# Attention heads sorted to partitions by transfers instead of turns on TensorE, with a new written order of steps

## Chip, core, metric

One NeuronCore of a Trainium2 chip runs the whole program in one launch. The metric is the device time in microseconds of that launch. The engines are TensorE (PE, matmuls; PEld is its weight load), VectorE (DVE), ScalarE (ACT), GpSimd (POOL) and SyncE (SP), which here only issues DMAs.

## What is computed

Two layers over x of shape 4 x 512 x 128 (batch, tokens, channels). Each layer normalizes x and adds an attention and a feed-forward branch to it. Cut to what matters:

```python
xn = _layernorm(x)
x = x + L0_attn(xn) + L0_ffn(xn)     # L0_ffn: ln, causal attention, residual, ln, mixture of 8 experts (128 -> 512 -> 128)
xn = _layernorm(x)
x = x + L1_attn(xn) + L1_ffn(xn)     # L1_attn: not causal; L1_ffn: 8 experts (128 -> 128 -> 128), top 2
# each attention, 16 heads of 8 channels:
scores = einsum('bhqd,bhkd->bhqk', q, k) / sqrt(8)      # causal in the first two
attn = softmax(scores)
out = einsum('bhqk,bhkd->bhqd', attn, v)                # heads side by side: 128 channels
out = out @ w_out
```

So there are 3 attentions for each of 4 batch elements, 12 in all, named (b, u) here: u = 0 is L0_attn, u = 1 the attention inside L0_ffn (both causal), u = 2 is L1_attn.

## The kernel before

Everything stays in SBUF between load and store. The channels or the keys lie on the 128 partitions, 512 tokens on the free axis (TILES = 4 tiles of 128). Heads are handled in four quads of four; quads 2n and 2n + 1 share one accumulation, a pair.

A step is a tuple such as ("max", b, u, g, i, k). The string SCORE is an order written out by hand: each letter takes the next step of one of 13 chains, a digit gives its PSUM bank. `plan` unrolls it, and every engine walks through the same list in order and executes its part of each step; semaphores join the parts. The letters: A the front of a batch element (norms, turns, projections, L84), K stacking q and k for the score matmuls (SP's DMAs, L1075) and loading the experts, M the scores whose maximum VectorE takes (L484, L810), T the turn of these maxima and their DMA into q_stack (max_turn, L833, L497, L1103), S scores and their exp (L840, L717), V values (L857), H the steps on heads, F the middle of a batch element (norms, routing, projections of u = 2), G gates and the store, E and O the layer-0 experts in and out, I and J those of layer 1.

One attention after its scores: the values step (L857) multiplies the exps by v_ones, whose 25 columns for each head are 8 values, a column of ones and zeros (the odd head of a pair comes 16 rows lower). So sum_bank, bank 7, fills with 8 unnormalized values and the sum of exps for each of 8 heads. ScalarE copies it to head_sums (L738) after the second quad of the pair. Then the H steps:

- heads_turn, once for each pair: four TensorE transposes of head_sums (L884); VectorE takes reciprocals of the sums (L511) and multiplies them in (L515) into heads.
- heads_back, once for each attention: four transposes of heads (L892); VectorE copies them to headsT (L520).
- out_project: four matmuls with the output weights (L899), added by VectorE (L530).

Each matmul or transpose of 32-bit numbers shows as two instructions in the trace's timeline when a group is merged (x8 for four), except for transposes.

ScalarE does exp for scores (L730) and gelu for experts (L754); it loads a table (ACT_TABLE_LOAD) whenever it changes from one function to the other.

SP's queue holds, in the order of the plan: loads of x, the stacking DMAs (up to 12 of 128 KB for one attention, L1095 and L353), the max_turn copies (L1108, 32 KB each), the stores (L1114).

## Time and profile before

| | |
|---|---|
| runs of the program | 780.64, 783.39, 783.80 us; median 783.39 |
| the profiled execution | 779.85 us |
| its span, first to last instruction | 778.0 us |
| TensorE granted clock, mean | 0.99 |
| instructions | 16113 |
| DMA packets, bytes | 34427, 31.70 MB |

Busy shares overlap in time, since the engines run side by side. The chain of work is followed back from the last instruction, at each step to what released it. Where an engine sat idle, the profile names what ended the wait. "issue" is time for which the profile shows no wait.

### The profile page before, as it was taken

How to read it: one execution, taken by the hardware profiler on the slowest of the kernel's cores; microseconds unless marked ns; L12 is line 12 of the kernel's file. 1: busy time of each engine (PE TensorE's matmuls, PEld its weight loads, DVE VectorE, ACT ScalarE, POOL GpSimd, SP SyncE). 2: the span in 40 equal slices, each digit the busy share in tenths (PEclk: the TensorE clock that was granted, in tenths of full speed). 3: DMA queues.
4: the chain of work that ended last, by engine and by line, in shares of the span. 5: the costliest groups of instructions: out<-in, count | busy, mean ns of one | idle time of the engine just before them, and what ended most of it. 6: DMA issues, size and time to landing. Idle time of an engine off the chain costs nothing.

```text
span 778.0 us, 16113 instructions
## 1 busy us (share of the span) xinstructions
PE 730.4 (94%) x6352; PEld 400.1 (51%) x6352; DVE 586.6 (75%) x1161; ACT 499.7 (64%) x623; POOL 181.4 (23%) x421
## 2 busy tenths in 40 slices
PE   3687999999999999999999999999999999999998
PEld 2332455677535366556444446566544566743344
DVE  5896996466999887477898887764898743579984
ACT  5374765566687566756777764746687683377784
POOL 5163553012432002112451200020552000010000
PEclk9799999999999999999999999999999999999999
DMA  5364230000200200030120110030030000011000
GB/s 136 78 192 168 71 79 16 3 19 3 77 19 11 67 17 3 18 88 5 52 61 3 49 44 3 3 91 3 19 93 4 3 1 3 1 51 44 16 5 14
DMA packets 34427, 31.70 MB, mean 41 GB/s; under 512 B 10184, under 2 KB 33616, under 8 KB 33872
## 3 DMA queue, kind: packets, MB, share of 16 engines
q1 hardware_dynamic: 32624, 29.09, 13.4%
q10 hardware_dynamic: 1728, 1.57, 0.9%
q8 instruction: 51, 0.84, 0.5%
q14 instruction: 24, 0.20, 0.1%
HBM read 7.32 MB, written 1.05 MB: 11 GB/s over the span
## 4 chain that ended last, share of the span: by engine, by line
PE 74%; DVE 11%; ACT 9%; DMA 3%; issue 2%; ACTq 0%; SPq 0%; POOL 0%; DVEq 0%; POOLq 0%
PE psum L950 17%; PE psum L937 14%; PE psum L872 14%; PE psum L824 8%; PE psum L851 8%; DVE neg_max L492 6%; ACT probs L754 3%; PE psum L803 3%; ACT L754 2%; ACT probs L730 2%; ACT L730 2%; DMA q_stack<-maxT 1%; PE psum L806 1%; PE psum L829 1%; PE psum L884 1%
## 5 line engine op out<-in xcount | busy, mean ns | idle before, releaser
L492 DVE TENSOR_REDUCE neg_max<-psum 128x2 f32<-128x1024 f32 (+2 forms) x320 | 344.9, 1111 | 87.2 <-PE psum L829 59.7
L730 ACT ACTIVATE probs<-psum 128x1024 f32<-128x1024 f32 (+1 forms) x320 | 288.5, 938 | 118.2 <-PE psum L851 116.7
L872 PE MATMUL psum<-probs,v_ones 128*25 128x512 f32 (+3 forms) x1536 | 152.3, 494 | 0.1
L754 ACT ACTIVATE probs<-psum,col 128x512 f32<-128x512 f32 x160 | 98.8, 688 | 53.3 <-PE psum L937 52.9
L824 PE MATMUL psum<-k_stack,q_stack 64*128 64x512 bf16 (+3 forms) x768 | 114.9, 331 | 15.4 <-ACT probs L730 4.2
L950 PE MATMUL psum<-ew,probs 128*128 128x128 f32 x1024 | 128.6, 279 | 0.0
L950 PEld LDWEIGHTS psum<-ew,probs 128*128 128x128 f32 x1024 | 120.3, 192 | 15.8 <-issue 13.5
L851 PE MATMUL psum<-q_stack,k_stack 64*128 64x512 bf16 (+3 forms) x768 | 108.2, 328 | 10.5 <-DMA q_stack<-maxT 4.9
L937 PE MATMUL psum<-normed_T_a,ew 128*128 128x512 f32 x256 | 117.2, 597 | 0.0
L1031 POOL TENSOR_SCALAR_AFFINE_SELECT probs<-probs 128x512 f32<-128x512 f32 x128 | 80.9, 640 | 145.7 <-ACT probs L730 144.1
L653 DVE SCALAR_TENSOR_TENSOR acc<-psum,gate,acc 128x128 f32<-128x128 f32 x256 | 72.1, 344 | 36.1 <-PE psum L950 32.3
L1017 POOL CAST max_part<-neg_max 128x16 bf16<-128x16 f32 x48 | 9.4, 196 | 352.2 <-DVE neg_max L492 352.1
L824 PEld LDWEIGHTS psum<-k_stack,q_stack 64*128 64x128 bf16 x768 | 37.1, 94 | 88.1 <-DVE neg_max L492 22.0
L851 PEld LDWEIGHTS psum<-q_stack,k_stack 64*128 64x128 bf16 x768 | 32.1, 94 | 76.0 <-ACT probs L730 25.3
L937 PEld LDWEIGHTS psum<-normed_T_a,ew 128*128 128x128 f32 x256 | 45.6, 190 | 46.2 <-issue 39.9
L754 ACT ACT_TABLE_LOAD x29 | 37.2, 1283 | 32.9 <-PE psum L937 32.7
L872 PEld LDWEIGHTS psum<-probs,v_ones 128*25 128x25 f32 x1536 | 33.5, 103 | 48.1 <-issue 31.5
L829 PEld LDWEIGHTS psum<-above,pick 64*128 64x128 bf16 x1024 | 44.4, 96 | 16.8 <-issue 1.0
L829 PE MATMUL psum<-above,pick 64*128 64x64 bf16 x1024 | 51.8, 192 | 0.0
L730 ACT ACT_TABLE_LOAD x26 | 33.4, 1283 | 26.0 <-PE psum L851 25.8
L950 PE MATMUL psum<-wout,probs 128*128 128x128 f32 x256 | 35.4, 283 | 0.5 <-ACT probs L754 0.5
L950 PEld LDWEIGHTS psum<-wout,probs 128*128 128x128 f32 x256 | 30.9, 191 | 8.2 <-issue 5.2
(126 smaller groups left out, 569.5 us busy)
## 6 DMA issues: line engine op xcount, KB each, us to landing
q_stack<-part SPq DMA_DIRECT2D x72, 128.0 KB, 2.4
k_stack<-part SPq DMA_DIRECT2D x60, 128.0 KB, 2.5
ew<-w_expert_in SPq DMA_DIRECT2D x1, 2048.0 KB, 8.1
ew<-w_expert_out SPq DMA_DIRECT2D x1, 2048.0 KB, 12.5
q_stack<-k_stack SPq DMA_DIRECT2D x14, 128.0 KB, 2.3
k_stack<-part ACTq DMA_DIRECT2D x12, 128.0 KB, 3.9
q_stack<-maxT SPq DMA_DIRECT2D x48, 32.0 KB, 1.9
x_in<-x SPq DMA_DIRECT2D x4, 256.0 KB, 3.4
```

Of the source, the lines that this page charges most:

```text
L492: eng.tensor_reduce(neg_max[:, q % 2, :, xs[0]:xs[-1] + 1, i], src, AX_X, ALU.max, negate=True).then_inc(vector_done.sem, 1)
L653: eng.scalar_tensor_tensor(out=acc_of[b % 2][:, t, :], in0=src[:, t * P:(t + 1) * P], scalar=gate_of[layer][:, t, expert:expert + 1], in1= ...
L730: eng.activation(dst, src, ACT.Exp, scale=SCALE).then_inc(probs_ready.sem, 1)
L754: ins = eng.activation(probs[:, order.slot[step[:-1]], 2 * k + f, :], two_banks(step)[:, f, :], ACT.Gelu_apprx_tanh if layer else ACT.Gelu ...
L803: ins = eng.matmul(dst, proj_qk[:, u, k, :], src[:, :], start=True, stop=True)
L824: ins = eng.matmul(dst[:, a, col0:col0 + keys], q_stack[slot][rows_of, head, i * P:(i + 1) * P], k_stack[slot][rows_of, head, 0:keys], sta ...
L829: ins = eng.matmul(dst[:, a, col0:col0 + HALF], pick[rows_of, upper, :], above[rows_of, upper, :], start=False, stop=upper == 1)
L851: ins = eng.matmul(dst[:, a, n * width:(n + 1) * width], k_stack[slot][rows_of, head, j * P:(j + 1) * P], q_stack[slot][rows_of, head, TIL ...
L872: ins = eng.matmul(sum_bank[32 * c:32 * c + V_COLS, q0:TILES * P], v_ones[u][:, j, g // 2 * QH + c, col0:col0 + V_COLS], probs[:, order.sl ...
L937: ins = eng.matmul(dst[:, f, :], w, normed_T["y" if layer else "a"][:, :], start=True, stop=True)
L950: ins = eng.matmul(dst[:, t * P:(t + 1) * P], middle[:, f, t * P:(t + 1) * P], w, start=f == chunks[0], stop=f == chunks[-1])
L1031: eng.affine_select(out=diagonal, in_=diagonal, compare_op=ALU.is_ge, fill=no_chance, base=0, pattern=[[0, QH], [1, P]], channel_multiplie ...
```

## The change

The turns of heads go. The columns of v_ones are laid out anew: each head has 16 rows of the sum bank (VALUE_ROWS), its 8 values at even rows and its sum of exps at row 1; 32 columns are loaded for each head (V_COLS) instead of 25, and the rows that it doesn't own are zeros. With that, values and sums of all heads lie at even strides over the partitions, and transfers can sort them:

- heads_sort, once for each pair: SP issues two DMAs from head_sums, the sums into heads_den (64 partitions x 64) and the values into heads_raw (64 partitions x 512, already in the order of channels).
- heads_inverse, once for each attention: VectorE waits for both pairs' sorts and takes one reciprocal over heads_den, 128 x 64.
- heads_write and heads_read: SP writes heads_den to a scratch in DRAM (16 x 512) and reads it back with each row spread over 8 partitions, into heads_inv (128 x 512).
- heads_norm: VectorE waits for the read and multiplies heads_raw by heads_inv into headsT.
- out_project is as before.

ScalarE's copy to head_sums now waits for the sorts of two pairs before. SCORE is written anew throughout; H has 84 steps instead of 48, the other chains have the same steps as before. The diff, without the string:

```diff
-SUM_COL, ODD_ROW = HD, 16
-ODD_COL = SUM_COL + 1 + ODD_ROW
-V_COLS, PAIR_COLS = ODD_COL, ODD_COL + SUM_COL + 1
+VALUE_ROWS, SUM_COL = 2 * HD, 1
+V_COLS, PAIR_COLS = 2 * VALUE_ROWS, 3 * VALUE_ROWS
...
-        heads += [("heads_turn", b, u, pair) for pair in range(QUADS // 2)] + [("heads_back", b, u), ("out_project", b, u)]
+        heads += [("heads_sort", b, u, 0), ("heads_sort", b, u, 1), ("heads_inverse", b, u), ("heads_write", b, u),
+                  ("heads_read", b, u), ("heads_norm", b, u), ("out_project", b, u)]
...
-        heads = sb("heads", [P, TILES, P])
-        inv_sum = sb("inv_sum", [P, TILES, 2 * QH])
+        heads_raw = sb("heads_raw", [P, TILES * P])
+        heads_den = sb("heads_den", [P, HALF])
+        heads_inv = sb("heads_inv", [P, TILES * P])
+        inverses = nc.dram_tensor("inverses", [HEADS, TILES * P], F32).ap()
...
-                        dst = v_ones[u][:, :, :, ODD_COL * odd:ODD_COL * odd + HD]
+                        dst = v_ones[u][:, :, :, V_COLS * odd:V_COLS * odd + VALUE_ROWS:2]
...
-                elif kind == "heads_turn":
-                    eng.wait_ge(vector_done.sem, vector_done.n)
-                    eng.reciprocal(inv_sum[:, :, :], src[:, :, :, SUM_COL]).then_inc(vector_done.sem, 1)
-                    eng.wait_ge(vector_done.sem, vector_done.count())
-                    eng.tensor_tensor(dst, src[:, :, :, 0:HD], inv, ALU.mult).then_inc(vector_done.sem, 1)
-                elif kind == "heads_back":
-                    eng.tensor_copy(headsT[:, :], bank(step)).then_inc(vector_done.sem, 1)
+                elif kind == "heads_inverse":
+                    n_heads = ATTENTIONS.index(step[1:])
+                    for pair in range(QUADS // 2):
+                        eng.wait_ge(heads_landed[pair].sem, 32 * (n_heads + 1))
+                    eng.reciprocal(heads_den[:, :], heads_den[:, :]).then_inc(vector_done.sem, 1)
+                elif kind == "heads_norm":
+                    eng.wait_ge(inverses_read.sem, 16 * (ATTENTIONS.index(step[1:]) + 1))
+                    eng.tensor_tensor(headsT[:, :], heads_raw[:, :], heads_inv[:, :], ALU.mult)\
+                       .then_inc(vector_done.sem, 1)
...
-                        eng.wait_ge(work_full.sem, order.work["heads_turn", *order.head_pairs[q - 2]] + 1)
+                        eng.wait_ge(heads_landed[q % 2].sem, 32 * (q // 2))
...
-                        col0 = (SUM_COL + 1) * (g % 2)
+                        col0 = VALUE_ROWS * (g % 2)
...
-                elif kind == "heads_turn":
-                    for t in range(TILES):
-                        ins = eng.transpose(dst[:, t * P:(t + 1) * P], head_sums[:, q % 2, t * P:(t + 1) * P],
-                                            ident[:, :])
-                elif kind == "heads_back":
-                    for t in range(TILES):
-                        ins = eng.transpose(dst[:, t * P:(t + 1) * P], heads[:, t, :], ident[:, :])
...
+                elif kind == "heads_sort":
+                    u, pair = step[2:]
+                    q = order.head_pairs.index((b, u, pair))
+                    if q >= 2:
+                        eng.wait_ge(vector_done.sem, order.dve["heads_norm", *ATTENTIONS[q // 2 - 1]])
+                    eng.wait_ge(scalar_done.sem, order.act["values", b, u, 2 * pair + 1, TILES - 1])
+                    rows_of = slice(HALF * pair, HALF * pair + HALF)
+                    for dst, src in ((heads_den, head_sums[SUM_COL:P:VALUE_ROWS, q % 2, :]),
+                                     (heads_raw, head_sums[0:P:2, q % 2, :])):
+                        eng.dma_start(dst[rows_of, :], src).then_inc(heads_landed[pair].sem, 16)
+                        heads_landed[pair].count()
+                elif kind == "heads_write":
+                    eng.wait_ge(vector_done.sem, order.dve["heads_inverse", *step[1:]])
+                    eng.dma_start(inverses, heads_den[:, :]).then_inc(inverses_written.sem, 16)
+                    inverses_written.count()
+                elif kind == "heads_read":
+                    eng.wait_ge(inverses_written.sem, 16 * (ATTENTIONS.index(step[1:]) + 1))
+                    eng.dma_start(heads_inv[:, :], inverses.unsqueeze(1).to_broadcast([HEADS, HD, TILES * P]))\
+                       .then_inc(inverses_read.sem, 16)
+                    inverses_read.count()
```

## Rows read from the trace of the kernel before

**Rows 1.** The page, part 1: busy us, share of span, instructions.

```profile
PE 730.4 (94%) x6352; PEld 400.1 (51%) x6352; DVE 586.6 (75%) x1161; ACT 499.7 (64%) x623; POOL 181.4 (23%) x421
```

**Rows 2.** The chain that ended last, shares of the span: engines, then lines.

```profile
PE 74%; DVE 11%; ACT 9%; DMA 3%; issue 2%; ACTq 0%; SPq 0%; POOL 0%; DVEq 0%; POOLq 0%
...
PE psum L950 17%; PE psum L937 14%; PE psum L872 14%; PE psum L824 8%; PE psum L851 8%; DVE neg_max L492 6%; ACT probs L754 3%; PE psum L803 3%; ACT L754 2%; ACT probs L730 2%; ACT L730 2%; DMA q_stack<-maxT 1%; PE psum L806 1%; PE psum L829 1%; PE psum L884 1%
```

**Rows 3.** Windows: PE, PEld, DVE, ACT, POOL busy us (instructions); clock, DMA share, GB/s.

```profile
0.00:40.00 40.00, 20.10 (x164) 11.28 (x164) 28.77 (x68) 18.05 (x35) 14.07 (x44) 0.87 0.46 109
...
80.00:120.00 40.00, 39.16 (x512) 19.61 (x515) 38.35 (x72) 28.83 (x37) 20.73 (x42) 1.00 0.26 68
```

**Rows 4.** Groups by form: busy us, mean ns of one | idle before.

```profile
L950 PE MATMUL psum<-ew,probs 128*128 128x128 f32 x1024 | 128.6, 279 | 0.0
...
L653 DVE SCALAR_TENSOR_TENSOR acc<-psum,gate,acc 128x128 f32<-128x128 f32 x256 | 72.1, 344 | 36.1 <-PE psum L950 32.3
...
L515 DVE TENSOR_TENSOR heads<-psum,inv_sum 128x256 f32<-128x256 f32 x24 | 10.2, 424 | 0.8
L511 DVE RECIPROCAL inv_sum<-psum 128x32 f32<-128x32 f32 x24 | 8.6, 357 | 9.9 <-PE psum L884 7.7
L520 DVE COPY headsT<-psum 128x512 f32<-128x512 f32 x12 | 8.2, 684 | 2.4 <-PE psum L892 2.4
```

**Rows 5.** VectorE's prices: groups by form, and line 594 (min/median/max ns).

```profile
L492 DVE TENSOR_REDUCE neg_max<-psum 128x2 f32<-128x1024 f32 x192 | 228.5, 1218 | 43.8 <-PE psum L824 25.1 <-PE psum L829 17.0
...
L417 DVE TENSOR_TENSOR acc<-x_bias,a_sum 128x512 f32<-128x512 f32 x4 | 2.7, 680 | 0.0
...
L594 DVE RECIPROCAL gate_t<-gate_s x4: 177/178/179, 214.2 to 742.5; 128x4 f32<-128x4 f32 x4
```

**Rows 6.** Pieces of the chain in order: start us, us, what.

```profile
92.64 0.59 PE psum L892 x4
...
112.76 0.61 DVE headsT L520
```

**Rows 7.** Weight loads: two groups by form, and one piece of the timeline.

```profile
L872 PEld LDWEIGHTS psum<-probs,v_ones 128*25 128x25 f32 x1536 | 33.5, 103 | 48.1 <-issue 31.5 <-POOL probs L1031 4.1 <-ACT probs L730 2.2
...
L790 PEld LDWEIGHTS psum<-ident,normed_a 128*128 128x128 f32 x16 | 1.7, 140 | 2.9 <-DVE normed_a L408 2.9
...
767.03 0.12 PEld L872 LDWEIGHTS psum<-probs,v_ones 128*25 128x25 f32 x4 [0.30 <-issue]
```

**Rows 8.** Groups: ScalarE's table loads ahead of gelu.

```profile
L754 ACT ACT_TABLE_LOAD x29 | 37.2, 1283 | 32.9 <-PE psum L937 32.7
```

**Rows 9.** Line 1108's issue (ns) and landing; then KB each, median us to landing.

```profile
L1108 SPq DMA_DIRECT2D q_stack<-maxT x48: 531/532/1263, 33.1 to 756.3; - x48
...
DMA to landing us min/median/max: 1.8/1.9/10.7
...
k_stack<-part SPq DMA_DIRECT2D x60, 128.0 KB, 2.5
...
q_stack<-maxT SPq DMA_DIRECT2D x48, 32.0 KB, 1.9
x_in<-x SPq DMA_DIRECT2D x4, 256.0 KB, 3.4
out<-acc SPq DMA_DIRECT2D x4, 256.0 KB, 2.6
```

**Rows 10.** The chain's end, in order of time: start us, us, what.

```profile
765.80 3.61 PE psum L872 x32
...
769.43 0.61 ACT head_sums L738
...
772.43 0.89 PE psum L950 x8
...
773.36 1.14 PE psum L899 x8
...
774.60 0.69 DVE acc L530
```

86 lines of the change are left out of this document (38 added, 48 removed).

## Prediction

> **What bounds the kernel now.** I read the busy shares first. TensorE is busy 730.4 us of 778.0 (94%), VectorE 75%, ScalarE 64% [rows 1]. Then the chain that ended last: 74% of it lies on TensorE, 11% on VectorE, 9% on ScalarE, 3% on DMA [rows 2]. So an instruction taken from TensorE's queue has about three chances in four of shortening the run. The stretches show where not: in the first 40 us TensorE is busy 28.77 us, held by loads and by the first chain of norm, projection and stacking, which the change leaves as it is; from 80 to 120 us VectorE is busy 38.35 of 40 us and TensorE merely follows it [rows 3]. The rest of the run is TensorE's, with small waits for PSUM banks.
>
> The profiled execution took 779.85 us, for a span of 778.0; the median of the runs shown is 783.39, a factor of 1.0045. The sum is made against 779.85 and multiplied by that factor at the end.
>
> **TensorE work removed.** Each of the 12 attentions turns its sums twice (L884, four transposes each) and its heads back once (L892): 24 + 12 = 36 groups. Four transposes take 0.59 us of the chain where nothing delays them [rows 6], so 36 x 0.59 = 21.2 us of TensorE's time go, and nothing on TensorE replaces them. Are they on the path? Going through the chain piece by piece, 28 of the 36 groups are on it, for 15.7 us, the tail's among them; [rows 6] has the first of L892's. The tail I count apart, so 14.4 us are proven on the path of the old order and at most 33 x 0.59 = 19.5 us can be had before the tail. The order is written anew around the missing groups, so I take 17, nearer the middle. **Term: -17 (-14.4 to -19.5).**
>
> **VectorE work.** Removed: 24 reciprocals of 0.357, 24 products of 0.424, 12 copies of 0.684 = 8.6 + 10.2 + 8.2 = 27.0 us [rows 4]. Added for each attention: one reciprocal over 128x64 and one product over 128x512. Reciprocals take 178 ns for 4 elements and 357 for 32 [rows 4, 5], 6.4 ns an element, so 0.56 us for 64; a tensor-tensor of 128x512 in SBUF takes 0.68 [rows 5]. 12 x 1.24 = 14.9 us. VectorE is relieved by 12.1 us. Its removed pieces lie on the chain for only 2.5 us (such as the 0.61 of headsT, [rows 6]), so at the same share the added work costs 1.4. **Term: -1.1 (-12.1 if VectorE ruled everywhere; 0 if hidden).** The copies into v_ones now write every second element; from their row's 24 instructions I see no reason for more than a few tenths of a us in all.
>
> **Wider value columns.** Weight loads for values go from 25 to 32 columns. 25 columns take 103 ns, 128 columns of the transposes 140 [rows 7], so 7 columns are 2.5 ns and 1536 loads 3.9 us. In a step of 512 queries they are hidden: after each four loads the loader idles 0.30 us [rows 7]. Only the narrow causal steps can show it. The matmuls stream the same queries. **Term: +1 (0 to +3.9).** The larger clears of v_ones (1536 elements instead of 1088 for each partition) fall in the first 40 us, some tenths.
>
> **Table loads.** ScalarE reloads its table at every change between exp and gelu, 55 times at 1.28 us (29 ahead of gelu in [rows 8], 26 ahead of exp). Following the steps scores, gate_exp and expert_in through both orders, the changes number 55 before and 49 after. On the chain the table loads (the pieces of L754 and L730 without a tile's name) stand with 2% each of 778 us, 2.1 and 1.6% before rounding: 29 us [rows 2], 0.52 us each, so six fewer give **-3.1 (0 to -7.7).**
>
> **The transfers, between the attentions.** The turns of an attention are replaced by six DMAs: two sorts for each pair of quads, one write, one read, all issued from SP. Issuing one holds SP 0.53 to 0.6 us [rows 9]; 72 more are some 43 us of a queue that is mostly waiting. None is nothing in time to landing: the sort of values moves 128 KB between SBUF rows as k_stack<-part does (2.5 us), the sort of sums and the write are small (32 KB of maxT in rows of 256 bytes takes 1.9; a write to DRAM, out<-acc, 2.6), the read of 256 KB is like x_in<-x (3.4) [rows 9]; I take 2.2 for the write and 2.9 for the read, a little below these rows since only the data of 32 KB come from DRAM. From the last values step to heads_inverse: copy 0.60, one issue 0.6 ahead of the second sort, landing 2.5: 3.7 us. From heads_inverse to heads_norm: 0.56 + 2.2 + 2.9 and three hand-overs of 0.1, about 5.9 us. VectorE executes in order, so what it has between these steps in the new order is the cover. By mean durations of its rows (a max over 1024 is 1.22, an expert's accumulation 72.1 / 64 = 1.13, [rows 4, 5]) the cover is, for the first gap and the second: attention (0,1) 4.1 and 5.5; (1,1) 3.6 and 4.9; (3,1) 3.6 and 5.6; (0,0) 5.3 and 6.5; (2,2) 4.5 and 10.0; (2,1) 14 and 8.4; (2,0) has 2.6 in the first gap, but two expert_in steps of TensorE pass there too, and 30 in the second; the four others have at least 5.4 and 11.5. So three attentions lack up to 1 us in each gap, the others next to nothing. ScalarE may reach the copy behind an exp of 1 us. A stall of VectorE at heads_inverse or heads_norm holds all max reductions behind it, and TensorE waits for their banks. **Term: +2.5 (0 to +12)**: the high end is each of the three transfers landing 1 us later at five attentions, most of it on the path.
>
> SP also executes in order. heads_write waits for VectorE and heads_read for the write's landing, and behind them stand max_turn copies, which scores wait for: behind the read of (0,1) and the write of (0,2) at once. These copies must pass a wait of about 2 us; scores of that quad follow several steps later. The old trace has such a wait once at its start (the DMA of maxT behind others: 10.7 us at worst against 1.9, [rows 9]), so the price is inside the +12 and no term of its own.
>
> The Trainium skill, "DMA: Bandwidth & Descriptors", sections "Specifications" and "Anatomy of one DMA", speaks against this change: rows under 512 B go through a read-modify-write, and completion is slowest where the target is HBM. The new sums and the scratch move in rows of 256 bytes, and the scratch is HBM. The trace does not show much of it: maxT's 256-byte rows land in 1.9 us, and the store to DRAM in 2.6. With the page's figure of about 2.0 us fixed for any DMA, an estimate from that page puts the three landings at 6 us instead of my 7.6 and the gaps' term near 0.
>
> **The tail.** Before: the last values end at 769.4 and the last sum at 775.3, 5.9 us [rows 10]. After, by the same rows and those above: copy 0.61, issue 0.6, sort 2.5, inverse 0.56, write 2.2, read 2.9, product 0.68, output projection 1.14, sum 0.69, six hand-overs of 0.1: 12.5 us, so +6.6. But seven expert_out steps stand behind the last values step instead of one, and a route_turn too: 6 x 0.97 + 0.44 = 6.3 us of TensorE work that ran before it; 81% of such work is on the chain (L950: 17% of 778 is 132 us, of 128.6 + 35.4 busy in its two forms; [rows 2, 4]), so -5.1. VectorE has 8.7 us of work ahead of heads_norm in the tail, less than the 9.9 to that point, so the transfers set the end. **Term: +1.5 (0 to +5).**
>
> **Sum.** -17 - 1.1 + 1 - 3.1 + 2.5 + 1.5 = -16.2; 779.85 - 16.2 = 763.7; times 1.0045 = 767.1 us.
>
> **Rivals.** (a) *The new order gains more than it loses work.* VectorE's 12.1 us also count in the stretches it rules, the groups are all worth their 0.59 and the waits are covered: -19.5 for the groups, -5 for VectorE, -4 for tables and fewer bank waits, +2 = -26.5, 757 us. For it: 47.6 us of TensorE idle stand in [rows 1], for an order to use. Against it: 11 of these are in the first 40 us [rows 3], where a dependency holds. (b) *The gain turns into other waits.* VectorE and ScalarE end next; TensorE's place on the chain passes to max reductions (6% now) and exps. Then only VectorE's relief and the tables count: -1.1 - 3.1 and a third of the groups, -6, with +3 of waits: -7, 776 us with the factor. For it: stretches like 80 to 120 us. Against it: 28 of 36 groups on the chain. (c) *The round trip is too long: slower.* One mechanism: VectorE stands at heads_norm (and SP at heads_read) until write and read have landed. It costs nothing up to about 6 us and then its excess at each tightly placed attention: (1,1), (3,2), (0,1), (3,1), (0,0) and, from 8.4 us, (2,1). With write and read each at twice their nearest row it is 10.8 us; the covers of 4.9, 5.2, 5.5, 5.6, 6.5 and 8.4 us lack 28.7 us together, at 0.85 on the path 24 us. Without the term for waits the sum is -18.7, so the result is 785, with the factor 789 us. It decides from about 10 us. For it: no row has a read of DRAM right behind a write of it, and 128 rows of 256 bytes to DRAM are not in the trace; one maxT copy took 10.7 us when others were ahead. Against it: the medians, and that stacking bursts rarely coincide. (d) *The change doesn't do what it says*: the shorter work only moves slack, the new order holding TensorE at banks for as long as the turns took, within 4 us of before: 782 us.
>
> **How the numbers follow.** Forecast (762 to 772) 0.45; (a) 0.22; (b) 0.14; (c) 0.13; (d) 0.06. About 0.5% (4 us) is what a measurement of this kernel can tell from no change, so faster needs less than 779.5: forecast, (a), and most of (b), 0.79; same 0.09, slower 0.12. The range leaves out half of (c) and the far end of (a): 753 to 785.
>
> **What would show it.** L884, L892, the copy and the small reciprocals gone; TensorE busy near 709 us; VectorE near 575; 51 or fewer table loads in all; the new transfers at 2 to 3.4 us; VectorE's waits for DMA ahead of heads_inverse and heads_norm below 5 us in total; last values to the end about 12.5 us plus the store. A read of the scratch at over 5 us, or VectorE's DMA waits over 15 us, would make the prediction wrong on the slow side; a chain below 70% on TensorE would point to (b).

## Result and profile after: slower by half a per cent

The changed kernel takes 786.75 us (median of 16 runs, 784.37 to 790.83) against 783.17 for the kernel before on the same chip (16 runs, 780.64 to 785.1): a ratio of 1.0047 with a 95% interval of 1.0034 to 1.006. The forecast was 767.1 us in a range of 753 to 785, so both the sign and the range were missed. The profiled execution took 787.67 us for a span of 785.8, at a mean granted clock of 0.969; the one profiled of before had 0.99. Times in the following sections are medians, each with its ratio to runs of the kernel before on the same chip; a few executions, of the kernel before too, took 17% to 125% longer than the others and are left out.

**Time goes with the granted clock.** TensorE's granted clock differs from run to run. Of 77 runs of the kernel before that stood beside the experiments, the 16 at a mean of 0.975 or 0.976 took 784.0 to 785.9 us, the 5 at 0.990 or 0.991 took 779.6 to 780.0: about 3.3 us for 0.01. (The profiled run of before is one of the high ones, so its busy times are not quite comparable with those of the others, which lie near 0.98.) The median clock is 0.980 over the runs of before and 0.976 over those of the changed kernel. By an estimate from these runs that is some 1.3 of the 3.6 us between them; what follows shows where a part of the low clock comes from.

The first row of the page of the changed kernel, busy us of each engine:

```profile
PE 723.4 (92%) x6208; PEld 386.7 (49%) x6208; DVE 574.7 (73%) x1126; ACT 487.8 (62%) x617; POOL 182.3 (23%) x421
```

The chain that ended last, its shares by engine:

```profile
PE 68%; DVE 10%; ACT 9%; DMA 3%; issue 2%; POOL 0%; SPq 0%; ACTq 0%; DVEq 0%
```

The 144 transposes are gone (6352 instructions to 6208, [rows 1]), VectorE's busy time fell by 11.9 us as forecast (12.1), ScalarE's by 11.9. TensorE's fell by 7.0 only, to 723.4 us where the prediction looked for 709. The span grew by 7.8 all the same. TensorE's share of the chain fell from 74% [rows 2] to 68%.

**One place shows at once.** SP's timeline (start us, us, queue, line, what) has the load of the experts' weights, four DMAs, and eight us behind it, with seven stacking transfers in between, a copy of maxima:

```profile
68.24 0.58 SPq L1060 DMA_DIRECT2D ew<-w_expert_in  x1
68.88 0.44 SPq L1060 DMA_DIRECT2D ew<-w_expert_out  x1
69.36 0.43 SPq L1060 DMA_DIRECT2D win<-w_in  x1
69.84 0.58 SPq L1060 DMA_DIRECT2D wout<-w_out  x1
...
78.08 1.02 SPq L1114 DMA_DIRECT2D q_stack<-maxT  x1
```

The same place in its chain (start us, us, what):

```profile
78.08 11.99 DMA q_stack<-maxT
```

In its waits (engine and line <- for what: us in total, times, longest):

```profile
PE psum L854 <- DMA q_stack<-maxT: 11.8, 1, 11.8
```

Its windows there (busy us and instructions of PE, PEld, DVE, ACT, POOL; clock, DMA share, GB/s):

```profile
70.00:80.00 10.00, 8.22 (x117) 3.29 (x117) 8.99 (x12) 6.41 (x9) 6.46 (x15) 1.00 0.97 399
80.00:90.00 10.00, 0.00 (x0) 0.00 (x0) 0.00 (x0) 0.00 (x0) 0.00 (x0) 0.55 1.07 252
90.00:100.00 10.00, 9.58 (x121) 3.85 (x121) 7.64 (x9) 5.84 (x7) 3.26 (x8) 0.77 0.33 79
```

From 80 to 90 us no compute engine did anything at all. The DMA engines were full with 5 MB of weights and the stacking transfers issued behind them, and a copy of 32 KB that usually lands in 1.8 us took 12.0. The granted clock was 0.55 in this stretch and 0.77 in the ten us behind it. The kernel before has the same load and a copy of 10.7 us [rows 9], but the load is issued at 50.6 us there, between other work, and TensorE waited 4.9 us for the copy. The new order moved the load to stand ahead of the stacking for the next batch element and of the copy for quad (0,1,1).

**What grew elsewhere.** Five more of the changed kernel's waits:

```profile
ACT probs L733 <- PE psum L854: 124.9, 131, 14.0
ACT probs L757 <- PE psum L923: 75.7, 39, 8.7
DVE neg_max L499 <- PE psum L832: 69.7, 44, 12.4
DVE acc L653 <- PE psum L936: 66.7, 28, 9.3
...
ACT L757 <- PE psum L923: 45.1, 17, 7.8
```

The first three in the kernel before:

```profile
ACT probs L730 <- PE psum L851: 116.7, 146, 5.3
DVE neg_max L492 <- PE psum L829: 59.7, 38, 5.8
ACT probs L754 <- PE psum L937: 52.9, 31, 5.2
```

The fourth stood at 32.3 there [rows 4], the last at 32.7 [rows 8]. The waits of ScalarE and VectorE for the experts' matmuls (second, fourth and fifth) grew by 38% to 107%. The stall above is in none of these three (none of their single waits is as long as it); it is in the longest of the other two, 14.0 and 12.4 us.

**What the transfers took.** The changed kernel's DMA issues (KB each, median us to landing):

```profile
heads_inv<-inverses SPq DMA_DIRECT2D x12, 256.0 KB, 3.3
...
inverses<-heads_den SPq DMA_DIRECT2D x12, 32.0 KB, 1.5
```

Line 1102, the write:

```profile
DMA to landing us min/median/max: 1.4/1.5/2.5
```

The reciprocal of line 517 (ns, first and last start, form):

```profile
L517 DVE RECIPROCAL heads_den<-heads_den x12: 539/544/554, 92.6 to 774.2; 128x64 f32<-128x64 f32 x12
```

The wait for the sorted sums and values:

```profile
DVE heads_den L517 <- DMA heads_raw<-head_sums: 2.1, 3, 1.0
```

The round trip is 1.5 + 3.3 = 4.8 us (5.1 forecast), and VectorE waited 2.1 us in all at the inverses and 0.6 at heads_norm. In the output projections TensorE's matmuls waited 2.2 us for headsT and its weight loads 3.1.

### The profile page after: what moved, and what is told of

The parts are those of the page before. It is cut to its first block, busy times and chain, and to the rows that moved or that the text cites. A ratio compares the mean times of both kernels' runs of the same rounds, so it can differ in the third digit from the quotient of the medians.

```text
span 785.8 us, 15828 instructions
## 1 busy us (share of the span) xinstructions
PE 723.4 (92%) x6208; PEld 386.7 (49%) x6208; DVE 574.7 (73%) x1126; ACT 487.8 (62%) x617; POOL 182.3 (23%) x421
## 4 chain that ended last, share of the span: by engine, by line
PE 68%; DVE 10%; ACT 9%; DMA 3%; issue 2%; POOL 0%; SPq 0%; ACTq 0%; DVEq 0%
PE psum L936 18%; PE psum L923 15%; PE psum L875 13%; PE psum L827 7%; PE psum L854 7%; DVE neg_max L499 4%; ACT probs L733 3%; PE psum L806 3%; ACT probs L757 2%; ACT L757 2%; DMA q_stack<-maxT 2%; DVE acc L653 1%; PE psum L832 1%; ACT L733 1%; PE psum L809 1%
## 5 line engine op out<-in xcount | busy, mean ns | idle before, releaser
L875 PE MATMUL psum<-probs,v_ones 128*32 128x512 f32 (+3 forms) x1536 | 159.0, 505 | 0.0
L827 PE MATMUL psum<-k_stack,q_stack 64*128 64x512 bf16 (+3 forms) x768 | 117.8, 340 | 18.1 <-ACT probs L733 5.9
L854 PE MATMUL psum<-q_stack,k_stack 64*128 64x512 bf16 (+3 forms) x768 | 110.3, 334 | 20.0 <-DMA q_stack<-maxT 11.8
L936 PEld LDWEIGHTS psum<-ew,probs 128*128 128x128 f32 x1024 | 120.0, 192 | 15.0 <-issue 12.9
L936 PE MATMUL psum<-ew,probs 128*128 128x128 f32 x1024 | 126.9, 278 | 0.4 <-ACT probs L733 0.4
L854 PEld LDWEIGHTS psum<-q_stack,k_stack 64*128 64x128 bf16 x768 | 32.3, 94 | 96.4 <-ACT probs L733 29.7
L757 ACT ACT_TABLE_LOAD x24 | 30.8, 1283 | 45.3 <-PE psum L923 45.1
L875 PEld LDWEIGHTS psum<-probs,v_ones 128*32 128x32 f32 x1536 | 34.2, 109 | 46.9 <-issue 31.5
L832 PE MATMUL psum<-above,pick 64*128 64x64 bf16 x1024 | 53.6, 195 | 0.0
L982 POOL TENSOR_TENSOR rstd<-var_eps,minus_half 128x4 f32<-128x4 f32 x16 | 16.2, 1013 | 84.6 <-DVE var_eps L403 84.3
## 6 DMA issues: line engine op xcount, KB each, us to landing
ew<-w_expert_out SPq DMA_DIRECT2D x1, 2048.0 KB, 12.8
```

The source lines that it names most:

```text
L757: ins = eng.activation(probs[:, order.slot[step[:-1]], 2 * k + f, :], two_banks(step)[:, f, :], ACT.Gelu_apprx_tanh if layer else ACT.Gelu ...
L827: ins = eng.matmul(dst[:, a, col0:col0 + keys], q_stack[slot][rows_of, head, i * P:(i + 1) * P], k_stack[slot][rows_of, head, 0:keys], sta ...
L832: ins = eng.matmul(dst[:, a, col0:col0 + HALF], pick[rows_of, upper, :], above[rows_of, upper, :], start=False, stop=upper == 1)
L854: ins = eng.matmul(dst[:, a, n * width:(n + 1) * width], k_stack[slot][rows_of, head, j * P:(j + 1) * P], q_stack[slot][rows_of, head, TIL ...
L875: ins = eng.matmul(sum_bank[32 * c:32 * c + V_COLS, q0:TILES * P], v_ones[u][:, j, g // 2 * QH + c, col0:col0 + V_COLS], probs[:, order.sl ...
L936: ins = eng.matmul(dst[:, t * P:(t + 1) * P], middle[:, f, t * P:(t + 1) * P], w, start=f == chunks[0], stop=f == chunks[-1])
```

## Experiments

Three questions: was it the experts' load; was it the transfers; and what was the removed TensorE work worth at all?

**1. The experts' load earlier in the changed kernel.** Half of it goes out when the first keys have landed (22.5 us), half behind the first max_turn (31.9 us); its place in the order is the only other difference. This kernel is called version 1 below.

```diff
-        "K": stacks[:2 * PARTS] + [("load_experts", 0)] + stacks[2 * PARTS:],
+        "K": stacks[:PARTS] + [("load_experts", 0)] + stacks[PARTS:3] + [("load_experts", 1)] + stacks[3:],
...
-                    for dst, src in ((ew1[:, :, :, :], w_expert_in), (ew2[:, :, :, :], w_expert_out),
-                                     (win[:, :, :], w_in), (wout[:, :, :], w_out)):
+                    if b == 0:
+                        eng.wait_ge(keys_landed[0].sem, 96)
+                    for dst, src in (((ew1[:, :, :, :], w_expert_in), (win[:, :, :], w_in)),
+                                     ((ew2[:, :, :, :], w_expert_out), (wout[:, :, :], w_out)))[b]:
```

> The changed kernel, but the experts' weights (5 MB) are asked for earlier: half once the first keys have landed (about 23 us), half after the first max_turn (about 31 us), instead of all at 68 us, ahead of the stacking of (1,0) and of the second max_turn of (0,1). Theory A (the late load is the largest loss of the start): the copy of maxT at 78 us no longer takes 12 us, TensorE's 12 us stall and the half clock right behind it go, and the kernel takes about 775 us, 1.5% under the changed kernel. Rival B (the stall only moves: the order behind it has the same slack in any case): 784 to 787 us. Rival C: the loads now collide with the first max_turn copies at 31 and 42 us, the gain is half of A's, 781 us.

> The changed kernel with the earlier load of the experts once more, for its interval: its undisturbed runs gave 772.3 and 774.1 us, and the two kernels that share its load and leave out transfers gave 776.2 and 773.4. Expected 775 us, 1.0% under the kernel before and 1.5% under the changed one; if the gain of the load were chance, 784 or more.

Measured: 772.26 and 774.06 us the first time, ratio 0.988 (0.9813 to 0.9946); 774.44 us (six runs, 772.79 to 776.09), ratio 0.9882 (0.9859 to 0.9905), the second. Against the changed kernel as it was that is 0.9882 / 1.0047 = 0.9836, 12.9 us, a little more than the one stall of 12. The rows of version 1, here and below, are from the second set. Its chain by engine:

```profile
PE 72%; DVE 13%; ACT 8%; DMA 3%; issue 2%; ACTq 0%; POOL 0%; SPq 0%; DVEq 0%; POOLq 0%
```

The load in SP's timeline:

```profile
22.53 0.36 SPq L1062 DMA_DIRECT2D ew<-w_expert_in  x1
...
31.93 0.59 SPq L1062 DMA_DIRECT2D ew<-w_expert_out  x1
```

Its waits:

```profile
PE psum L854 <- DMA q_stack<-maxT: 2.6, 2, 2.4
...
ACT probs L757 <- PE psum L923: 75.6, 39, 8.7
DVE acc L653 <- PE psum L936: 66.7, 28, 9.3
```

The wait for maxima fell from 11.8 us to 2.6; the waits for the experts' matmuls are what they were, so they are not what the 12.9 us were made of. The expected 775 us came. This kernel is faster than both others.

**2. The same edit in the kernel before,** and a variant with the whole load at once as soon as the first keys have landed (its diff against the version in halves):

```diff
-                    for dst, src in (((ew1[:, :, :, :], w_expert_in), (win[:, :, :], w_in)),
-                                     ((ew2[:, :, :, :], w_expert_out), (wout[:, :, :], w_out)))[b]:
+                    for dst, src in ((ew1[:, :, :, :], w_expert_in), (ew2[:, :, :, :], w_expert_out),
+                                     (win[:, :, :], w_in), (wout[:, :, :], w_out)):
```

> The kernel before with the same earlier load as after_early, as a control. In the kernel before the copy of maxT at 56 us lands after 10.7 us behind the load and TensorE idles for about 5 us. Theory A: that wait goes and the kernel takes 778 us, 0.7% under the kernel before; the gain of the same edit is thus larger in the changed kernel. Rival B: no change, 782 to 784 us.

> The kernel before with the whole load of the experts asked for once the first keys have landed (23 us). In before_early the second half of the load stood ahead of the second max_turn copy, which took 10.6 us. Here the load should have landed by 38 us, ahead of that copy at 41.6, at the price of up to 4 us for the first copy at 33. Theory A (only the copies behind the load matter): 773 to 775 us, the stall of 6 us gone too. Rival B (the stall comes out elsewhere, VectorE setting the pace up to 60 us): 778 us as before_early.

Measured: in two halves 778.11 us, 0.9943 (0.9923 to 0.9963), theory A's time but, as its chain shows below, not for theory A's reason; all at once 780.66 us, 0.9963 (0.9948 to 0.9979), outside what either theory of that run expected. So 4.5 us of the 9.2 that version 1 is ahead of before have nothing to do with the heads. The chain of the version in halves still has one late copy:

```profile
41.80 10.63 DMA q_stack<-maxT
```

TensorE waited 6.2 us for it, more than the 4.9 in before; in the other variant it waited 3.5 us, and that one is not faster (the two intervals overlap). In this kernel the length of that wait and the time of the run do not go together, so what the 4.5 us are made of stays open. In the changed kernel they do, in experiments 1 and 4.

**3. The load from another queue.** Is it SP's queue order or the DMA engines that hold the copy? ScalarE issues the load, at the same place of the order.

```diff
+                elif kind == "load_experts":
+                    for dst, src in ((ew1[:, :, :, :], w_expert_in), (ew2[:, :, :, :], w_expert_out),
+                                     (win[:, :, :], w_in), (wout[:, :, :], w_out)):
+                        eng.dma_start(dst, src).then_inc(experts_loaded, 16)
```

> The changed kernel with the experts' load at its place in the order, but issued from ScalarE's queue instead of SP's. Theory A (order within SP's queue is what holds the copy of maxT): the copy passes by, lands in 2 to 4 us, and the kernel takes about 777 us, near the 774.4 of the earlier load. Rival B (any 5 MB in flight fill the 16 engines): the copy still takes 8 to 12 us and the kernel takes 785 to 788 us.

Measured: 786.3 us, 1.0045 (1.0026 to 1.0064), the same as the changed kernel's 1.0047. ScalarE's timeline has the load's last part at 66 us:

```profile
66.03 1.07 ACTq L719 DMA_DIRECT2D wout<-w_out  x1
```

The chain has the copy:

```profile
74.56 12.78 DMA q_stack<-maxT
```

The copy is issued 7.5 us after the issue of the load's last part has ended (7.7 in the changed kernel), with nothing of the load in its own queue, and takes 12.8 us. Theory A of this run fails: which queue issues the megabytes makes no difference. What holds the copy then, the load itself or the stacking transfers of 128 KB that stand ahead of it in its own queue and are slowed by the load, this run doesn't separate. The Trainium skill, "DMA: Bandwidth & Descriptors", section "Queues, rings and completion order", has each DMA engine take turns between the queues at the granularity of a packet, by which the small copy should pass most of the load from another queue; this run doesn't show that, with the reservation just made. The section "Issuing engines are not separate DMA queues" of that page says that SP's and ScalarE's queues share the same 16 engines, and with that the run agrees.

**4. The clock at the start.** The changed kernel's granted clock is lower from 0 to 40 us. Its first two windows:

```profile
0.00:20.00 20.00, 6.69 (x20) 3.57 (x20) 11.92 (x47) 11.92 (x21) 9.86 (x33) 0.90 0.54 139
20.00:40.00 20.00, 14.28 (x137) 6.76 (x141) 16.44 (x20) 5.19 (x16) 2.30 (x9) 0.50 0.09 21
```

That is 0.70 in the mean against 0.87 [rows 3]: all of the second stretch ran at 1.2 GHz. Filler matmuls on the identity between the first steps keep TensorE busy there, with the load late and early:

```diff
+        idle = {"project": 0, "max": 2, "turn": 10}
+                count = 8 if step == ("project", 0, 0, 2) else 2 if step == ("turn", 0, "x") else idle[step[0]]
...
+                for _ in range(count):
+                    eng.matmul(sum_bank.rearrange("p (a b) -> p a b", a=TILES), ident16[:, :],
+                               ident16[:, :].unsqueeze(1).to_broadcast([P, TILES, P]), start=True, stop=True)
```

> The changed kernel with filler matmuls (bf16, 128x512, into the still unused sum bank, nobody reads them) on TensorE where it waits up to the first values step: 2 after the first turn, 8 after the values' projection, 10 after the second turn, 2 after each max step. Its early half-clock stretch, 16 to 43 us in the profile, should disappear. Theory A (the early half clock costs what TensorE's steps took longer, some 1 us each at two projections and the first values step): 3 us gained, 783 to 784 us. Rival B (VectorE's max reductions set the pace there at any clock): within 1 us of 786.75. Rival C: the fillers stand in the way of the max steps, 2 to 4 us slower.

> The earlier load of the experts and the fillers together. The earlier load alone ran 772.3 and 774.1 us. Theory A (two separate losses): about 770 us. Rival B (the clock is nothing): 772 to 774. As this kernel has the load moved too, it also repeats that result: over 780 would say that the gain of the earlier load was chance.

Measured: 791.05 us, 1.0123 (1.0082 to 1.0165), with the mean clock of its profiled execution at 0.979 instead of 0.969; with the load early 777.38 us, 0.9933 (0.9912 to 0.9954), clock 0.996. Both are slower than the same kernel without fillers, and the second is outside all that was expected of it. Over its runs the median clock rose from 0.982 to 0.993, worth some 3.6 us by the relation in the result's section, and the time rose by 4.0 us instead, so the fillers themselves would cost some 7 us; this is an estimate from these runs. The low clock of the first 40 us is not where most of the time went: version 1, 13 us faster than the changed kernel, has a granted clock of 0.50 there too, from 20 to 30 us. In the first of the two the copy behind the load held TensorE for 15.2 us (11.8 without fillers), and between the two lie 1.0123 - 0.9933, 15 us: once more the length of that stall.

**5. The transfers taken away,** from version 1. First the write and the read (the values are then squared instead of normalized), then all of them (the values of attention don't reach the output projection; reciprocal and product run on other data).

```diff
-                    eng.wait_ge(inverses_read.sem, 16 * (ATTENTIONS.index(step[1:]) + 1))
-                    eng.tensor_tensor(headsT[:, :], heads_raw[:, :], heads_inv[:, :], ALU.mult)\
+                    eng.tensor_tensor(headsT[:, :], heads_raw[:, :], heads_raw[:, :], ALU.mult)\
...
-                    eng.dma_start(inverses, heads_den[:, :]).then_inc(inverses_written.sem, 16)
-                    eng.dma_start(heads_inv[:, :], inverses.unsqueeze(1).to_broadcast([HEADS, HD, TILES * P]))\
```

> The changed kernel with the earlier load, without heads_write and heads_read: heads_norm multiplies the raw values by themselves, so the softmax is not normalized; the sorts, the reciprocal and all other steps stay. It prices the round trip through DRAM. Theory A (it is covered, apart from what the profile shows: VectorE waited 0.6 us for it and TensorE 5.3 us for headsT): 0 to 4 us under the kernel with the earlier load, 769 to 773 us. Rival B (the missing gain sits in the round trip): 760 us or less.

> The same, with the sorts left out as well: no transfer of heads at all, heads_inverse and heads_norm work on a tile that is long there (normed_T_x), heads_inverse still waiting for the last copy of the sums; the attention's values don't reach the output. This is the floor of this order with transfers that cost nothing. Theory A (transfers are covered; the missing gain is in the order, that is in waits for banks and exps): 767 to 772 us. Rival B (transfers, SP's queue and the waits cost what is missing): 755 to 760 us.

Measured: 776.23 us, 0.9914 (0.9885 to 0.9943), and 773.38 us, 0.9885 (0.985 to 0.992), against 0.9882 (0.9859 to 0.9905) with all transfers; neither median falls below the version with all transfers by more than 1.1 us, so neither theory A nor rival B of either text came out. The intervals overlap; from 0.985 to 0.9905, their far ends, all 72 DMAs and their waits cost at most 4.3 us, and by the medians nothing. That leaves room for the prediction's term of 2.5 us and none for rival (c)'s 24: the round trip is covered.

**6. Each set of instructions in the other's order.** The kernel before with the new order (turns where the transfers stood), and the changed one with the old order. Of the first the last line of the order is shown:

```diff
-6S0S4VM2M0J6S4S2VJ0S4S2T6J1J6S4S2VS0S4J6VS2S0S4J6G2VS0S4S2VVVVH6H2G3H6J2H6G
+0S2H6S0GS4VT6S2S0G6S4GVS2S0VS4S2VS0VH6S4S2GJ6S0VVVJ6J0H4G1H5J2G6J3J2J6J3H6G
```

> The kernel before (turns on TensorE, all its instructions) walked through in the new order: each of the two turns stands where the sort of that pair stood, heads_back stands where the write of the inverses stood, each with the PSUM bank that is longest unused. It has the new order's place for the experts' load. Theory A (replacing the turns is worth what TensorE's path says, and the new order is what costs): 786.75 + 17 = about 804 us. Rival B (the turns were hidden in slack and transfers gain nothing in this order): 786 to 791 us.

> The changed kernel's instructions in the order of before: the sorts stand where the turns stood, heads_inverse about 3.5 us of VectorE and ScalarE work later, write at once, read and norm as far behind as the steps that use the result allow. For the attentions (b,1) nothing stands between inverse and output projection that could cover the round trip. Theory A (removing the turns saves 17 us, an uncovered round trip of about 6 us at four attentions and the tail gives back 20 to 30): 785 to 795 us. Rival B (transfers gain in any order, since other engines' work covers them): 768 to 773 us.

Measured: 838.1 us, 1.0706 (1.0648 to 1.0765), and 834.75 us, 1.0676 (1.062 to 1.0733), both far outside what was expected. Waits of the second:

```profile
PE psum L885 <- DVE headsT L521: 25.6, 6, 7.8
DVE headsT L521 <- DMA heads_inv<-inverses: 16.7, 7, 4.9
```

Here the transfers stand uncovered and cost what they take. Crossed in this way, the two kernels take some 55 and 53 us more than before. In both the steps were put in by rule and not fitted, so how much of this another placement would win back is not shown. These two runs therefore say nothing on what order and instructions contribute each, which is what they were meant for; the next ones were made for it, leaving the order of before as it is.

**7. What the turns are worth in before.** Twice each; shrunk to one transpose of 32x32 for each group (the output then isn't the attention's); and with no step on TensorE at all (likewise). Of each edit one place is shown.

```diff
-                    for t in range(TILES):
+                    for t in (*range(TILES), *range(TILES)):
```

```diff
-                    for t in range(TILES):
-                        ins = eng.transpose(dst[:, t * P:(t + 1) * P], heads[:, t, :], ident[:, :])
+                    ins = eng.transpose(dst[0:32, 0:32], heads[0:32, 0, 0:32], ident[0:32, 0:32])
```

```diff
-        singles = {"turn", "project", "max_turn", "heads_turn", "heads_back", "out_project", "route", "route_turn",
+        singles = {"turn", "project", "max_turn", "out_project", "route", "route_turn",
```

> The kernel before with each of its 36 groups of four transposes (24 of head_sums, 12 of heads) done twice on TensorE, nothing else changed: 21.2 us of TensorE's work added at the places from which the change takes it. Theory A (TensorE's time at these places is the path, as the prediction held with 28 of 36 groups on the chain): +16 to +21 us, about 801. Rival B (the order has slack behind these places): +5 to +10 us, about 790.

> The kernel before with each group of four 128x128 transposes shrunk to one of 32x32, so that nearly all of TensorE's 21.2 us go while every step, bank, wait and VectorE instruction stays (VectorE reads the untransposed sums from SBUF instead, its reciprocals are of a constant, so the attention's values are wrong). Theory A (work taken from the chain comes off the time): -14 to -18 us, about 766. Theory B (an order fitted to the turns gives back less than it costs to add: TensorE arrives earlier and waits longer for banks and exps): -5 to -9 us, about 776.

> The kernel before, where TensorE takes no part in heads_turn and heads_back at all: no transposes, no waits, no banks. VectorE does its three operations on SBUF data instead (values wrong, as in before_turns_tiny). Theory A (VectorE and ScalarE hold the time, TensorE's turns sit in slack): within 3 us of before_turns_tiny, 779 to 783 us. Theory B (what counted in the turns were their waits for the copy and their banks): 768 to 773 us.

Measured: twice 794.09 us, 1.0142 (1.011 to 1.0175), +11 us; tiny 781.92 us, 0.9974 (0.9957 to 0.9991), -2 us, less than either theory; none 781.08 us, 0.9956 (0.9938 to 0.9975), -3.4 us. The groups of transposes in before:

```profile
L884 PE MATMUL psum<-ident,head_sums 128*128 128x128 f32 x96 | 15.2, 280 | 0.6 <-DVE x_bias L530 0.3
L892 PE MATMUL psum<-ident,heads 128*128 128x128 f32 x48 | 7.8, 285 | 0.0
```

The same, each done twice:

```profile
L884 PE MATMUL psum<-ident,head_sums 128*128 128x128 f32 x192 | 25.4, 276 | 0.5 <-DVE x_bias L530 0.3 <-ACT head_sums L738 0.2
L892 PE MATMUL psum<-ident,heads 128*128 128x128 f32 x96 | 13.0, 278 | 0.0
```

The page's first row of the tiny kernel:

```profile
PE 726.8 (93%) x6244; PEld 392.1 (50%) x6244; DVE 585.4 (75%) x1161; ACT 499.7 (64%) x623; POOL 183.4 (24%) x421
```

Its chain by engine:

```profile
PE 68%; DVE 15%; ACT 11%; issue 2%; DMA 2%; ACTq 0%; POOL 0%; DVEq 0%; POOLq 0%
```

This is the step that failed. Without the turns' time the chain has 6 points less of TensorE, 4 more of VectorE and 2 more of ScalarE than in [rows 2]: 6% of 778 or some 47 us of TensorE left it, of which the groups were 15.7, and other engines' work took their place.

The doubling added less than was expected of it: four more transposes right behind four cost 0.43 us (25.4 + 13.0 - 15.2 - 7.8 = 15.4 us of busy time for 36 groups), not the 0.59 that the first four take on the chain. So added work costs 11 of 15.4 us, 0.7 of its duration. Removed work gives back far less: 2.0 us where the groups' busy time fell from 23.0 to 7.1 us, 3.4 where it went altogether.

The clock is not what hides the gain. At a granted clock of 0.974 to 0.976 the tiny kernel took 781.9 to 783.4 us and before 784.0 to 785.9. It does blur the busy times: the tiny kernel's 726.8 us were taken at a clock of 0.980, where a kernel with all its turns (the variant of experiment 2 with the whole load at once) has 734.6, so TensorE's busy time fell by some 8 us and not by the 3.6 that [rows 1] suggests. The Trainium skill, "Perfetto Trace Analysis", section "Identifying the Most-Contended Engine", calls matmul busy time a bad measure of how close a kernel is to its limit, because pipelined matmuls look smaller in the trace. These runs don't show that reason; they show that 94% busy says little of what work taken away gives back.

**8. VectorE's part, alone and together.** VectorE's 27 us of head work cut down (one small reciprocal and one small copy are left of each; from the second attention on the output is wrong), and both this and no turns.

```diff
-                    eng.reciprocal(inv_sum[:, :, :], src[:, :, :, SUM_COL]).then_inc(vector_done.sem, 1)
+                    eng.reciprocal(inv_sum[:, :, 0], minus_half[:, :]).then_inc(vector_done.sem, 1)
...
-                    eng.tensor_copy(headsT[:, :], bank(step)).then_inc(vector_done.sem, 1)
+                    width = TILES * P if (b, step[2]) == (0, 0) else 8
+                    eng.tensor_copy(headsT[:, 0:width], bank(step)[:, 0:width]).then_inc(vector_done.sem, 1)
```

> The kernel before with TensorE's turns kept and VectorE's part of the heads (27 us of reciprocals, products and copies) cut to a few elements; values wrong. Theory A (several engines are jointly critical: relief of one gives little): 777 to 782 us. Rival B (VectorE is the true bound): 765 to 770 us.

> Both together: no turns on TensorE and nearly nothing on VectorE (values wrong). If the two engines are jointly critical, relief of both gives clearly more than the sum of the two alone: theory A 768 to 773 us against some 780 for each alone. Rival B (the order itself, its waits on exps and table loads, holds the time): 776 us or more.

Measured:

| kernel before, old order | TensorE's turns kept | without |
|---|---|---|
| VectorE's head work kept | 1 | 0.9956 (0.9938 to 0.9975) |
| cut | 0.9953 (0.9935 to 0.9972) | 0.9898 (0.9868 to 0.9927) |

In us: 3.4, 3.7, and 8.0 together (776.95 us). What is left of VectorE's head work in the light kernel:

```profile
L516 DVE COPY heads<-inv_sum 128x4 f32<-128x4 f32 x23 | 5.6, 242 | 0.8
L511 DVE RECIPROCAL inv_sum<-minus_half 128x4 f32<-128x4 f32 x24 | 4.3, 180 | 10.5 <-PE psum L886 8.5
L522 DVE COPY headsT<-psum 128x8 f32<-128x8 f32 x11 | 1.8, 162 | 3.0 <-PE psum L894 3.0
```

With two copies of full width it is 13 us, since a small instruction still takes 160 to 240 ns; so 14 of the 27 us were taken away and not all. That is about what the change takes too (12). The turns on TensorE and 14 us of VectorE's time, with no transfer in their place, are worth 8 us in this order.

The joint gain of 8.0 us (interval 5.7 to 10.3) is not clear of the sum of the two, 7.1. Theory A, that the two engines are jointly critical and relief of both gives clearly more than the sum, is thus not shown; 776.95 us is what rival B expected, that waits of the order itself hold the time. Which waits these are stays open. Chain of the kernel without both:

```profile
PE 68%; ACT 13%; DVE 12%; DMA 3%; issue 2%; POOL 1%; ACTq 0%; SPq 0%; DVEq 0%; POOLq 0%
```

Nearly a third of it is ScalarE's, VectorE's, transfers and hand-overs.

**9. The end of the old order.** Laid beside before by the work done, the changed kernel gains in the middle and loses some 6 us between 690 and 740 us (a rough reading, since the orders differ; from 700 to 730 us TensorE is busy 24.1 of 30 us in version 1 and 28.9 in before). Version 1 with its steps from about 675 us on in the order of before tries that, one expert_out left for the tail. Of the string's last three lines, the last:

```diff
-S0S2H6S0GS4VT6S2S0G6S4GVS2S0VS4S2VS0VHS4S2GJ6S0VVVJ6J0HG1HHJ2G6HJ3J2J6HJ3H6G
+J6S0S4VM2HM0J6S4S2VJ0S4S2T6J1J6S4S2VS0S4J6VS2S0S4J6G2VS0S4S2VVVVG3HJ2HHHHH6G
```

> The changed kernel with the earlier load, whose steps from about 675 us on stand in the order of before (with its banks), with transfers put in after the steps they need. Its tail has one expert_out step left to cover the last transfers instead of seven. Theory A (the new order pays for the tail's cover earlier: between 690 and 740 us VectorE's and ScalarE's steps lack these matmuls as company): 6 us are won there and the tail costs 6 us more, total within 3 us of 774.4. Rival B (the order of the end is merely worse): 768 us. Rival C (its loss is the table loads and clock, whatever the order): 780 us.

Measured: 783.4 us, 1.0001 (0.9982 to 1.002), 9 us slower than version 1. Its waits:

```profile
PE psum L885 <- DVE headsT L521: 8.3, 2, 8.0
DVE headsT L521 <- DMA heads_inv<-inverses: 5.3, 2, 4.8
```

8 of the 9 us are as long as that one wait of TensorE; where no expert work stands between the last values and the output projection, the transfers lie open. None of the three expectations was met (rival C's 780 us is the nearest). Why the new order loses between 690 and 740 us stays open: the experiment did not take that loss away (TensorE is busy 25.5 of the 30 us from 700 on). Where TensorE stands still there in version 1, it mostly waits for ScalarE's exps and gelus (4.9 us from 695 to 735 us, none in before).

## Why the prediction was wrong, step by step

**TensorE work removed: -17, the step that failed.** "28 of the 36 groups are on it, for 15.7 us", and so "14.4 us are proven on the path": this took the chain for the only path. Experiment 7 puts the removal at 2 to 3.4 us in the old order. The chain is one path through the run; when its work gets shorter, other waits take its place, as the shares in experiment 7 show. Here a share of the chain told roughly what adding work costs (0.7 of its duration), and was no more than an upper bound of what removing it gives. Which paths hold the time after the removal is not shown. Rival (d) was of this kind, and (b) named the sign to look for, a chain below 70% on TensorE; it came out at 68%. (b)'s 776 us is within 2 us of what the changed kernel takes once its load is out of the way (774.4), but in part by luck: 4.5 us of that are the earlier load's own, which (b) knew nothing of, and like for like the gain is 4.8 us against (b)'s 7.

One reading under this step is wrong. In [rows 3] the columns are TensorE, its weight load, VectorE: in the first 40 us TensorE is busy 20.1 us and idle 19.9, not busy 28.77 (that is VectorE's) and idle 11, and from 80 to 120 us it is busy 39.16 of 40 us and so does not merely follow VectorE's 38.35. No term uses these, but only 27.7 of the 47.6 idle us lie behind the start, less than rival (a) had for an order to use.

**VectorE work: -1.1, too small for its own effect but right in kind.** Its 11.9 us fell as worked out (reciprocal 544 ns against 560 forecast, product 681 against 680). Alone, 14 us of VectorE's head work were worth 3.7 us, as much as all of TensorE's turns.

**The step left out: the load of the experts.** The prediction saw the copy of 10.7 us in [rows 9] and took it for a wait behind other DMAs; but it put the price "inside the +12" of the transfers, and never asked what those others were (the load of the experts) and where load_experts stands in the new order. It cost 13 us. That the changed kernel's 786.75 us came near rival (c)'s 789 is chance: (c)'s mechanism is a round trip that VectorE stands waiting for; it takes 4.8 us and cost nothing that could be measured. ((c)'s 10.8 us is twice the prediction's own 2.2 and 2.9 and 0.56 for the reciprocal, not twice the nearest rows, which would be more.)

**The transfers: +2.5, not contradicted.** Landings of 1.5 and 3.3 us against 2.2 and 2.9; experiment 5 bounds the whole at 4.3. For the write to DRAM in rows of 256 bytes the fixed 2.0 us that the prediction cites from the Trainium skill ("DMA: Bandwidth & Descriptors") is more than the measured 1.5, so the warning about such rows didn't come true here. (The page gives the figure for the path of GpSimd's DMAs, and these are SP's. Its fit also adds the bytes at 436 GB/s, which the prediction left out: by an estimate from the page the three landings would be 7.0 us, not 6.)

**Table loads: -3.1, the count right, the worth unknown.** The changed kernel has 24 ahead of gelu (29 in [rows 8]) and 24 elsewhere, beside the first of all; 48 against 49 forecast, and before has 56 against the prediction's 55, so eight went and not six:

```profile
L757 ACT ACT_TABLE_LOAD x24 | 30.8, 1283 | 45.3 <-PE psum L923 45.1
```

But ScalarE's idle time ahead of those before the gelus rose from 32.9 to 45.3 us, more than eight loads of 1.28 us give back. No run prices the loads by themselves.

**Wider values: +1, not contradicted.** The weight load takes 109 ns against 103 [rows 7], 6 ns where 2.5 were estimated. The matmuls of the values are no longer for it: in the new order their mean is 505 ns with 25 columns (the first kernel of experiment 6) and 505 ns with 32.

**The tail: +1.5, length right and cause wrong.** From the end of the last values to the end of the last sum are 12.9 us (12.5 forecast, without the store). Pieces of the chain:

```profile
767.33 2.83 PE psum L875 x24
770.15 1.10 PE psum L936 x8
...
771.28 1.14 DVE acc L653 x4
...
774.23 0.56 DVE heads_den L517
...
779.30 1.13 DVE acc L653 x4
780.43 0.61 DVE headsT L521
...
782.34 0.69 DVE acc L530
```

From 771.3 us on VectorE's accumulations of the experts fill it almost without a gap, and the transfers run beside them: the last read, issued at 776.3 us, lands some 3.3 us later, 0.7 us before VectorE comes to headsT's product at 780.3. The prediction said that these 8.7 us would be less than the transfers' path of 9.9, and so that the transfers set the end.

**The balance.** With the load out of the way on both sides the changed kernel stands at 0.9882 / 0.9943 = 0.9939 of before, -4.8 us. Against the sum of -16.2 that is the turns' term, mis-sized by some 14 us by what experiment 7 measured in the old order, in part made up by the rest. The early load alone gives before 4.5 us, and its late place takes 12.9 from the changed kernel: -4.8 - 4.5 + 12.9 = +3.6 us, the measured 0.47%. What of -4.8 is the missing work and what the order's, the runs don't tell, since neither ran well without the other as they were crossed.

## To carry to other kernels

Before a gain is read off the chain, take the work away in a kernel whose output may be wrong, and see what the run gives back: with TensorE 94% busy and 74% of the chain, all its turns of heads (21 us by their price on the chain) were worth 3.4. When an order is written anew, list every step that moved, bulk loads first, and ask of each what small transfer is issued in the ten us behind it. A part of a change tried in the other's order, put in by rule, measures the misfit. And compare busy times only at about the same granted clock: one busy time taken at 0.990 beside one at 0.980 was off by 4 us here.

## What the runs showed of the hardware

- A copy of 32 KB, 1.8 us by itself, lands 12.0 us after its issue behind 5 MB of loads of the same queue, and 12.8 us when the load was issued 7.5 us earlier from another engine's queue; in both cases stacking transfers of 128 KB stood ahead of it in its own queue.
- A write of 32 KB to DRAM in 256-byte rows lands in 1.5 us, less than the same amount between SBUF rows (1.8), and a read of 256 KB from it, each row spread over 8 partitions, right behind it in 3.3.
- Four 128x128 transposes of 32-bit numbers take 0.59 us on the chain, and four more right behind them 0.43.
- Over 77 runs of one kernel the time went with TensorE's mean granted clock: 784.0 to 785.9 us at 0.975 or 0.976, 779.6 to 780.0 at 0.990 or 0.991.
- TensorE at 1.2 GHz through 20 us of the start was not mended with gain by these fillers: holding the clock up with them made both kernels slower, by 0.5 and 0.8% (0.9933 / 0.9882 and 1.0123 / 1.0047).
